# First layer's half gates spread over ScalarE, VectorE and GpSimd, and results read back sequence by sequence

## What is computed

```python
# layer 0, HIDDEN = 384
gate = jnp.einsum('bsd,hd->bsh', x, wg)
up = jnp.einsum('bsd,hd->bsh', x, wu)
h = jax.nn.silu(gate) * up
return jnp.einsum('bsh,dh->bsd', h, wd)
...
# layer 1, H = 256, comb holds the two weights of a token or 0
for e in range(E):
    g = jax.nn.silu(xf @ gate_proj_w[e].T)
    u = xf @ up_proj_w[e].T
    y = g * u @ down_proj_w[e].T
    out = out + comb[:, e:e + 1] * y
```

## Time and profile before

| | us |
|---|---|
| median of 3 runs | 530.15 |
| lowest and highest run | 530.13, 531.07 |
| the profiled execution | 527.27 |
| its span (first to last instruction) | 524.9 |
| TensorE (PE) matmuls busy | 452.6 (86%) |
| VectorE (DVE) busy | 400.5 (76%) |
| ScalarE (ACT) busy | 330.0 (63%) |
| GpSimd (POOL) busy | 262.3 (50%) |

### The profile page before, as it was taken

One profiled execution on the slowest core, in us unless ns is written; L12 is line 12 of the kernel. 1 busy time (PEld: TensorE's weight loads), 2 busy tenths in 40 slices (PEclk: granted clock), 3 DMA queues, 4 the chain that ended last, 5 costly groups with the idle time before them and its releaser, 6 DMA issues.

```text
span 524.9 us, 9470 instructions
## 1 busy us (share of the span) xinstructions
PE 452.6 (86%) x3442; PEld 175.6 (33%) x3442; DVE 400.5 (76%) x562; ACT 330.0 (63%) x434; POOL 262.3 (50%) x499
## 2 busy tenths in 40 slices
PE   3555989999999999999989888988999999999850
PEld 1201123324332443244324322321345545455510
DVE  4599889986998699969986987898887777633204
ACT  2201677775777677866785777767856665767550
POOL 6781075723535383788377757873202323253250
PEclk9855899999999999999999999999999999999995
DMA  3896439525720361545263635464720111010018
GB/s 85 232 235 101 76 125 262 173 113 175 148 105 2 124 64 19 64 145 61 24 71 121 79 34 68 142 76 63 88 65 29 46 44 51 11 43 25 16 61 213
DMA packets 143742, 48.27 MB, mean 92 GB/s; under 512 B 109890, under 2 KB 139090, under 8 KB 142866
## 3 DMA queue, kind: packets, MB, share of 16 engines
q1 hardware_dynamic: 141394, 42.93, 39.2%
q0 software_dynamic: 2304, 4.76, 2.7%
HBM read 22.81 MB, written 23.14 MB: 88 GB/s over the span
## 4 chain that ended last, share of the span: by engine, by line
PE 52%; DVE 18%; issue 9%; ACT 9%; SPq 6%; DMA 4%; POOL 1%; POOLq 0%; ACTq 0%; DVEq 0%
PE ps L779 13%; DVE mx L1147 12%; PE ps L763 9%; PE ps L748 7%; ACT PT L992 5%; SPq L446 4%; PE ps L828 4%; PE ps L820 3%; PE ps L709 2%; PE ps L821 2%; PE ps L803 2%; PE ps L843 2%; PE ps L840 2%; PE ps L804 2%; DMA h_all<-y_tokens 1%
## 5 line engine op out<-in xcount | busy, mean ns | idle before, releaser
L1147 DVE TENSOR_REDUCE mx<-ps 128x2 f32<-128x1024 f32 x256 | 307.6, 1221 | 58.6 <-PE ps L748 55.1
L992 ACT ACTIVATE PT<-ps 128x1024 f32<-128x1024 f32 x256 | 258.8, 1025 | 108.2 <-PE ps L763 101.7
L779 PE MATMUL ps<-PT,Vp 128*32 128x512 f32 x1024 | 137.2, 608 | 4.5 <-ACT PT L992 4.4
L748 PE MATMUL ps<-KO,QO 48*128 48x512 bf16 (+1 forms) x512 | 103.9, 404 | 33.8 <-ACT PT L992 15.7
L763 PE MATMUL ps<-QO,KO 59*128 59x512 bf16 x512 | 99.8, 388 | 1.8 <-DVE mx L1147 1.7
L536 POOL DMA_INDIRECT y_tokens<-expert_io,meta x40 | 38.5, 963 | 70.9 <-ACT expert_io L1027 48.1
L763 PEld LDWEIGHTS ps<-QO,KO 59*128 59x128 bf16 x512 | 24.5, 93 | 137.9 <-issue 74.6
L1169 DVE SCALAR_TENSOR_TENSOR th<-th,ps 128x320 f32<-128x320 f32 (+1 forms) x56 | 25.5, 455 | 32.0 <-ACT th L1012 31.6
L748 PEld LDWEIGHTS ps<-KO,QO 48*128 48x128 bf16 (+1 forms) x512 | 25.5, 95 | 63.5 <-ACT PT L992 29.6
L525 POOL DMA_INDIRECT x_places<-xe,place_i x32 | 31.9, 996 | 20.4 <-ACT PT L992 14.6
L561 POOL CAST mp<-mx 128x32 bf16<-128x32 f32 x16 | 3.4, 213 | 72.9 <-DVE mx L1147 69.0
(11 more groups left out here) (166 smaller groups left out, 485.9 us busy)
## 6 DMA issues: line engine op xcount, KB each, us to landing
z<-part SPq DMA_DIRECT2D x16, 384.0 KB, 2.6
z<-part SPq DMA_DIRECT2D x16, 256.0 KB, 3.0
QO<-z SPq DMA_DIRECT2D x64, 48.0 KB
KO<-z SPq DMA_DIRECT2D x64, 48.0 KB
x_places<-expert_io SPq DMA_DIRECT2D x2, 1300.0 KB, 7.2
expert_io<-x_places SPq DMA_DIRECT2D x8, 320.0 KB, 3.7
QO<-z SPq DMA_DIRECT2D x6, 384.0 KB
KO<-z SPq DMA_DIRECT2D x6, 384.0 KB
```

The source lines that it names most:

```text
L748: mm = pe.matmul(ps[:, 2 * pair + half, :], rows_of(QO[u % 3], half, 2 * s + jj, rows, (qt, qt + 1)), rows_of(KO[u % 3], half, 2 * s + jj, ...
L779: last = pe.matmul(ps[32 * g:32 * g + 32, PV_BANK, :], Vp[u % 2][:, k, head(s, g), :], PT[:, (2 * t + g % 2) % 4, g // 2, :], start=(s % 2 ...
L992: act.activation(PT[:, e % 4], ps[:, 2 * pair:2 * pair + 2, :], ACT.Exp).then_inc(exp_done, 1)
L1147: dve.tensor_reduce(mx[:, a, qt, col:col + 5:4], ps[:, 2 * pair:2 * pair + 2, :], AX_X, ALU.max, negate=True).then_inc(max_read, 1)
```

## The change

*Gates of layer 0.* ScalarE, after the tanh of a gate, also copies half of the up part (scale 0.5) from PSUM into the hidden rows (`up_copy`, semaphore `up_copied`). VectorE makes `(th + 1) * gate` only; for side gates it waits for the copy first. The second product, now without the factor, is made by GpSimd in SBUF (`gate_products`), at three places in its queue. The tanh has four places in turn (`th0`) and waits for the product four gates back. TensorE's waits for PSUM are now for VectorE's first product and for the copy; the output matmuls still wait for `h_ready[0]`.

*The end.* Sends of experts 3 to 7 don't wait for an exponential. A token's row in `y_tokens` is numbered by partition first, so that a sequence's results are 2 KB in a row for each partition. There are eight loads of 256 KB, two for each sequence, each sequence with a semaphore of its own. VectorE adds sequences 0 to 2, then the last residual, then sequence 3.

```diff
@@ sb
+        th0 = th[:].rearrange("p a (b n) -> p (a b) n", b=2)
@@ take_pair
-                left = {"score": exp_done, "max": max_read, "gate0": h_ready[0], "gate1": h_ready[1],
+                left = {"score": exp_done, "max": max_read, "gate0": gate_done[0], "gate1": h_ready[1],
                         "places": places_ready, "expert": y_copied}[before]
                 pe.wait_ge(left, m + 1)
+                if before == "gate0":
+                    pe.wait_ge(up_copied, m + 1)
@@ results_of, load_results, store
-            return t[:, 0:4 * NT * D].rearrange("p (k b t d) -> p k b t d", k=2, b=2, d=D)
+            return t[:, 0:4 * NT * D].rearrange("p (b k t d) -> p b k t d", k=2, b=2, d=D)[:, b % 2]
...
-                first = k * T + 2 * pair * S
-                src = y_tokens[first:first + 2 * S].rearrange("(b t p) d -> p b t d", b=2, p=P)
-                sp.dma_start(results_of(pair)[:, k], src).then_inc(y_in[pair], 16)
+                first = k * T + b * S
+                src = y_tokens[first:first + S].rearrange("(p t) d -> p t d", p=P)
+                sp.dma_start(results_of(b)[:, k], src).then_inc(y_in[b], 16)
...
-            if b < B - 1:
-                sp.wait_ge(result, b + 1)
-            else:
-                sp.wait_ge(unit_done, U)
+            sp.wait_ge(result, b + 1)
@@ send_results
-                pool.wait_ge(exp_done, 2 * result_slot(e) + 2 + j)
+                if e < 3:
+                    pool.wait_ge(exp_done, 2 * result_slot(e) + 2 + j)
@@ pool side
+        def gate_products(pool, u, pieces):
+            for g in range(GATES_U * u, GATES_U * (u + 1))[pieces]:
+                i, c = g % GATES_U // 2, g % 2
+                h = h0_T[:, i, c * (S // 2):(c + 1) * (S // 2)]
+                pool.wait_ge(gate_done[0], g + 1)
+                pool.wait_ge(up_copied, g + 1)
+                pool.tensor_tensor(h, h, th0[:, g % 4, :], ALU.mult).then_inc(h_ready[0], 1)
...
+            if u < B:
+                gate_products(pool, u, slice(0, 3))
             if n < U:
                 split_max(pool, n, 0)
+            if u < B:
+                gate_products(pool, u, slice(3, 4))
...
             if f < U and layer(f) == 1:
                 choose_experts(pool, f, route)
+            if u < B:
+                gate_products(pool, u, slice(4, 6))
@@ side_mms: slots 0, 10 and 15
-                pe.wait_ge(h_ready[0], ...)
+                pe.wait_ge(gate_done[0], ...)
+                pe.wait_ge(up_copied, ...)
@@ scalar side
+            if L == 0 and g >= 4:
+                act.wait_ge(h_ready[0], g - 3)
...
+        def up_copy(act, g):
+            _, up = gate_up_of(0, g)
+            i, c = g % GATES_U // 2, g % 2
+            act.wait_ge(up_ps[0], g + 1)
+            if g % GATES_U == 0 and g > 0:
+                act.wait_ge(y_ps, g // GATES_U)
+            act.activation(h0_T[:, i, c * (S // 2):(c + 1) * (S // 2)], up, ACT.Copy, scale=0.5).then_inc(up_copied, 1)
...
                     half_tanh(act, 0, g)
+                    up_copy(act, g)
@@ gated
+            if L == 0 and GATES[g % GATES_U][1] == "side":
+                dve.wait_ge(up_copied, g + 1)
             dve.wait_ge(tanh_done[L], g + 1)
             dve.scalar_tensor_tensor(out=t, in0=t, scalar=1.0, in1=gate, op0=ALU.add,
                                      op1=ALU.mult).then_inc(gate_done[L], 1)
+            if L == 0:
+                return
@@ residual, add_results, last_vector
-            if u == U - 1:
-                dve.wait_ge(result, B)
...
-            for b in range(B):
+            for b in range(B - 1):
                 add_results(dve, b)
             residual(dve, U - 1)
+            add_results(dve, B - 1)
@@ constants
-            pool.iota(dest_0[:], pattern=[[P, NT], [T, 2]], base=0, channel_multiplier=1,
+            pool.iota(dest_0[:], pattern=[[1, NT], [T, 2]], base=0, channel_multiplier=NT,
@@ sync
-            for pair in range(2):
-                load_results(sp, pair)
+            for b in range(B):
+                load_results(sp, b)
```

More of the change, by code:

```diff
@@ L227, in build @@
         h_ready = [sem(f"h_ready{i}") for i in range(2)]
+        up_copied = sem("up_copied")
         xn_twice = sem("xn_twice")
@@ L236, in build @@
         y_sent = [sem(f"y_sent{i}") for i in range(2)]
-        y_in = [sem(f"y_in{i}") for i in range(2)]
+        y_in = [sem(f"y_in{b}") for b in range(B)]
         first_added = sem("first_added")
@@ L377, in load_meta, with results_of, load_results @@
                 sp.dma_start(meta[:, e], src[:, e, :, D:ROW]).then_inc(meta_in, 16)
-        def results_of(pair):
-            t = (Vp[0][:].rearrange("p k h f -> p (k h f)"), h_all[:])[pair]
-            return t[:, 0:4 * NT * D].rearrange("p (k b t d) -> p k b t d", k=2, b=2, d=D)
-        def load_results(sp, pair):
-            if pair == 0:
+        def results_of(b):
+            t = (Vp[0][:].rearrange("p k h f -> p (k h f)"), h_all[:])[b // 2]
+            return t[:, 0:4 * NT * D].rearrange("p (b k t d) -> p b k t d", k=2, b=2, d=D)[:, b % 2]
+        def load_results(sp, b):
+            if b == 0:
                 sp.wait_ge(y_sent[0], 16 * JE * (E // 2))
@@ L865, in side_mms @@
                 pe.wait_ge(mT_ready, 2 * u + 1)
-                pe.wait_ge(h_ready[0], GATES_U * min(u, B))
+                pe.wait_ge(gate_done[0], GATES_U * min(u, B))
+                pe.wait_ge(up_copied, GATES_U * min(u, B))
                 qk_mm(pe, p, 0, SIDE)
@@ L905, in side_mms @@
                 if slot == 15:
-                    pe.wait_ge(h_ready[0], g)
+                    pe.wait_ge(gate_done[0], g)
+                    pe.wait_ge(up_copied, g)
                 gate_up_0(pe, g)
@@ L912, in side_mms @@
                 for g in gates_at(u, 9, "side"):
-                    pe.wait_ge(h_ready[0], g + 1)
+                    pe.wait_ge(gate_done[0], g + 1)
+                    pe.wait_ge(up_copied, g + 1)
                 out_transposes(pe, u, 0)
@@ L1007, in half_tanh @@
             act.wait_ge(gate_ps[L], g + 1)
[L1008 to L1012, removed]
+            if L == 0 and g >= 4:
+                act.wait_ge(h_ready[0], g - 3)
+            if L == 1:
+                act.wait_ge(*((h_ready[1], g - 1) if g >= 2 else (h_ready[0], GATES_U * B)))
+            act.activation(th0[:, g % 4, :] if L == 0 else th[:, g % 2, 0:n], gate, ACT.Tanh, scale=0.5).then_inc(
+                tanh_done[L], 1)
+        def up_copy(act, g):
[5 more added lines that the diff above has]
+            act.activation(h0_T[:, i, c * (S // 2):(c + 1) * (S // 2)], up, ACT.Copy, scale=0.5).then_inc(up_copied, 1)
         def places_copy(act, e):
@@ L1166, in gated @@
             n = S // 2 if L == 0 else HALF
-            t = th[:, g % 2, 0:n]
+            t = th0[:, g % 4, :] if L == 0 else th[:, g % 2, 0:n]
+            if L == 0 and GATES[g % GATES_U][1] == "side":
+                dve.wait_ge(up_copied, g + 1)
             dve.wait_ge(tanh_done[L], g + 1)
@@ L1170, in gated @@
                                      op1=ALU.mult).then_inc(gate_done[L], 1)
+            if L == 0:
+                return
             dve.wait_ge(gate_done[L], g + 1)
             dve.wait_ge(up_ps[L], g + 1)
[L1173 to L1183, removed]
-                dst = h1_T[:, e % 2, g % 4 // 2, g % 2 * HALF:(g % 2 + 1) * HALF]
+            e = g // 4
+            if g == 0:
+                dve.wait_ge(y_ps, B)
+            if g % 4 == 0 and e >= 2:
+                dve.wait_ge(expert_ps, e - 1)
+            dst = h1_T[:, e % 2, g % 4 // 2, g % 2 * HALF:(g % 2 + 1) * HALF]
             dve.scalar_tensor_tensor(out=dst, in0=t, scalar=0.5, in1=up, op0=ALU.mult,
@@ L1198, in add_results @@
             tile = out_tile(B + b)
-            dve.wait_ge(y_in[b // 2], 32)
-            if b < B - 1:
-                dve.wait_ge(unit_done, B + b + 1)
-            else:
-                dve.wait_ge(base_ready, U)
-            dve.tensor_tensor(tile[:], tile[:], results_of(b // 2)[:, 0, b % 2], ALU.add).then_inc(first_added, 1)
+            dve.wait_ge(y_in[b], 32)
+            dve.wait_ge(unit_done, B + b + 1)
+            dve.tensor_tensor(tile[:], tile[:], results_of(b)[:, 0], ALU.add).then_inc(first_added, 1)
             dve.wait_ge(first_added, b + 1)
-            dve.tensor_tensor(tile[:], tile[:], results_of(b // 2)[:, 1, b % 2], ALU.add).then_inc(result, 1)
+            dve.tensor_tensor(tile[:], tile[:], results_of(b)[:, 1], ALU.add).then_inc(result, 1)
         def read_logits(dve, u):
```

## The result

| | us |
|---|---|
| median of 20 runs, changed | 529.74 (525.07 to 531.22) |
| median of 20 runs, before, beside them | 530.98 (529.93 to 532.54) |
| ratio, with its 95% interval | 0.9966 (0.9953 to 0.998) |
| the profiled execution | 529.41, span 527.6 |
| TensorE, VectorE busy | 459.6, 391.4 |

The change is faster by 0.34%, about 1.8 us. That is less than half of the 4.4 us forecast, and 529.74 lies outside the range, above 528.6. The runs are spread unevenly: three have a mean granted clock of TensorE of 0.954 to 0.961 and took 525.07, 525.20 and 526.81 us; the other 17 have 0.942 to 0.948 and took 527.85 to 531.22.

The account below looks back on a forecast made before the run. TensorE was taken to pace the passes, and a chain of sends, loads, adds, residual and store the end. Gates +0.7 and end -5.1 gave -4.4 us, so 525.7 us, range 523.5 to 528.6.

Parts of the forecast that it names:

- step (c): Kernel end: VectorE's new order of adds and residual, paced from its normalization on, ends the span at 519.8, 5.1 us less.
- TensorE bounds the passes, VectorE's product removed: nothing: First-layer gates: VectorE's second product, 10.1 us in all, lies beside TensorE's work, so removing it was costed at nothing.
- ScalarE's copy, +0.7 us: First-layer gates: a copy taken at 0.382 us delays exponentials, 0.25 us a pass, +0.7 us after later waits take some back.
- GpSimd's product: First-layer gates: 24 products taken at 0.61 us, 14.6 us in all, covered in a queue idle half the time.
- (a): Kernel end: sends of experts 3 to 7 without their wait let the loads start 3.4 us earlier.
- (b): Kernel end: eight 256 KB loads keep the level 290 GB/s, with no gain taken for longer rows.
- From the profiled execution to the median, 2.9 us: Whole kernel: the runs' median, 530.15 us, stood 2.9 above the profiled 527.27, carrying the forecast from 522.9 to 525.7.
- (1): Gates pay as well, PSUM pairs coming back 0.4 us sooner: 2.5 us more gained, 522.5 us, chance 0.10.
- (3, 4): Gates cost 2 to 3.5 us through delayed exponentials, chance 0.12; or ScalarE's copy is exposed at every gate, 532.7, chance 0.07.
- Rival 2: Kernel end gains by its new order alone, something else holding the loads back: 528.6 us, chance 0.08.
- Rival 5: Kernel end: the small loads don't overlap, eight at 3.3 us each, about 542 us, chance 0.02.
- theory C: From the experiments: expert 7's results copied 0.6 us late in slot 11, last pass, tips TensorE's clock to half.

Follow-up runs that it names:

- e6: The kernel before, with no edit, profiled once more: 525.89 us, span 523.6.
- e9: The changed kernel, with no edit, run once more: 523.17 us, ratio 0.9932 to the kernel before.
- e3: Changed kernel plus three unused score products in each of slots 12 to 15 of the last pass and three ahead of the last value matmuls: 525.94 us, ratio 0.9912.
- e11: The kernel of e12 with the old gates put back, new end kept: 521.23 us, ratio 0.9894 to the kernel before.
- e7: The kernel before with only the waits of the sends of experts 3 to 7 removed: 523.64 us, ratio 0.9948.
- e12: Changed kernel, last pass: second scores ahead of value products in slots 13 to 15, two idle score products per slot in 12 to 15: 521.69 us, ratio 0.9895.
- e2: Changed kernel with the end undone, so new gates with the old end: 529.76 us, ratio 0.9981 to the kernel before.
- e1: Changed kernel with the gates undone, so old gates with the new end: 530.18 us, ratio 0.9982 to the kernel before.
- the first set: The follow-up kernels e1 to e4, run beside a kernel before with a median of 531.04 us.
- the third set: The follow-up kernels e9 to e12, run beside a kernel before with a median of 527.28 us.
- e10: Changed kernel with the waits for exponentials back ahead of the sends of experts 3 to 7: 525.28 us, ratio 0.9969 to the kernel before.
- e4: Changed kernel with second scores ahead of the value matmuls in slots 13 to 15 of the last pass: 525.28 us, ratio 0.9899 to the kernel before.

## Why the prediction was wrong

**What failed is step (c) of the end**, "What takes over is VectorE from its normalization on, which hangs on the last exponentials". The new bound was named rightly, but its time was read off one execution, in which the clock of TensorE stayed full until 513.6. The earlier trace rows gave a clock of 0.68 for the stretch from 507.4, and the step didn't ask at which matmul it fell, nor whether it always fell there. It doesn't: in the kernel before alone it fell at 513.6 once and at 500.8 once (e6). The old end hid that, since the loads came later than the last heads in either case. The new end hangs on the heads, and in 17 of 20 runs, by their mean clock, the fall came ahead of them. In numbers, from the slots of the two profiles: the tail behind slot 15 is 3.4 us shorter rather than 5.1 and slots 13 to 15 are 2.84 longer, which leaves 0.5 of 5.1. With the clock kept the 5.1 is there (e9), and its 4.1 us by the medians, or 3.6 by the ratio, is near the forecast of 4.4; e3, which changes nothing else than what TensorE does while it waits, gives 2.9 to 3.8 us back.

The Trainium skill, TensorE: Matmul & The Clock Gate, section HAM oscillation, tells of matmuls too short for the DMA that they wait for: in each wait TensorE loses its full clock and starts the next work cold. The trace agrees in direction only. Here the wait is for ScalarE, and no pause of TensorE in the 4 us before the fall is over 1.5 us. The page would have been the one to weigh against step (c).

Point by point:

- **TensorE bounds the passes, VectorE's product removed: nothing.** Right: 51.86 us busy in the third pass before and after.
- **ScalarE's copy, +0.7 us.** Duration right to 0.001 us. The effect was of the wrong sign: slots 9 and 14 lose 0.2 us each as the working has it for slot 9, but what slots 15 and 0 were to lose isn't there; slot 0 gives 0.22 back. It comes to about -0.1 us in the second and third pass and, beside e11, to -0.3 in the fourth, where 0.25 was taken for each.
- **GpSimd's product.** 0.73 us rather than 0.61, and covered all the same.
- **(a) Sends, 3.4 us.** Confirmed by the start of the first load in e7.
- **(b) Eight loads.** They overlap, and no add waits for one in the profiles of the change. With the last slots shortened they are the bound again (e12).
- **From the profiled execution to the median, 2.9 us.** Left unexplained in the prediction. In e2's profile 2.6 us of this kind lie in the passes 3 to 5 and the last one.

The rivals: gates that pay 2.5 us (1) or cost 2 or more (3, 4) are excluded by the passes and by e2's 0.4 to 1.6 us. Rival 2's 528.6 us lies nearest to the result, but its mechanism isn't there: the loads start 0.3 us earlier than in the profile of before although slot 12 ahead of them begins 3.1 us later. Rival 5, and with it the estimate of 20.8 us for eight loads one after another, is excluded by the transfer rates: all eight moved within 7 us. The case that happened was on no list.

**Open.** What sets the moment of the fall. By the mean clock it came early in 17 of 20 runs of the change and 11 of 12 of e1 in the first set, where every profile with the new end and free sends had slot 11 at 8.15 to 8.21 us, and in none of six in the third set (e9), where slot 11 took 7.56, by the same rough sign. That fits theory C but doesn't show it: e10 has early falls with a short slot 11, and e3 has a long slot 11 without an early fall. In the profiles of the kernel before and of e6 slots 11 to 13 are alike (7.57, 1.81 and 2.56 us), and yet the clock fell inside slot 13 in e6 and 13 us later in the other, so what TensorE does in these slots doesn't settle it alone. By the same sign the kernel before fell early in 6 of 23, 5 of 17 and 5 of 17 runs of the three sets. What delays ScalarE's copy by 0.62 us in slot 11, and what makes the gaps in the small matmuls, wasn't found either; neither could be switched on or off by an edit.

## What to carry to other kernels

Before a change moves the end of a kernel to another chain, read the granted clock in small windows along that chain, and in more than one execution: a stretch that nothing waited for may hide a clock that falls at a different place each time. Where the last matmuls wait for another engine, idle products can hold the clock (e3, 2.9 us by the ratios where it mostly fell early), and work moved forward can make the loop short enough that a fall costs less (e4, 3.6 us). If a profiled execution lies under all timed runs, look for the rows that make the difference before adding it to a forecast.

## What was not expected of the hardware

- The clock fell from 1.00 to 0.50 with TensorE busy for about half of the four microseconds before, without a pause of it over 1.5 us, and in the same kernel at 503.5 in one execution and at 512.6 in another, in which TensorE was half busy from 502 to 506 as well. An early fall cost 4.6 us of 525 between these two: 2.84 in three slots and 1.8 in the last transposes and output products.
- Twelve idle products in the stretch and three behind it (e3), on the last pass's operands, held it in the profile and, by the mean clock of 0.959 to 0.962, in all six executions, at no cost that shows.
- GpSimd's product of 128x256 in place, both inputs from SBUF, takes 0.73 us, its other operation of that shape 0.61.
- A burst of 128 matmuls of 32 columns can have a gap of 0.4 to 0.6 us with no releaser: in the profile of the change and in all four of the first set, and none over 0.25 us in the eight of the other two sets.
